# One causal-attention-and-experts kernel: scores by pairs of heads, transfers over two queues, later inverse deviations, fillers laid anew

## The reference, cut to what matters

```
x = x + skip(row_lstm(x))            # gated recurrence over the 16 rows, 48 features
t = tokens(x)                        # 16 images x 256 tokens x 96 channels
q, k, v = heads(ln(t) @ Wq, Wk, Wv)  # 6 heads of 16
s = (q . k) * 96**-0.5, causal       # 256 x 256 per image and head
t = t + (softmax(s) @ v) @ Wp + bp
g = softmax(ln(t) @ gate_w + gate_b), the best 2 of 4 kept and rescaled
t = t + sum_e g_e * (gelu(ln(t) @ w1_e + b1_e) @ w2_e + b2_e)    # 4 experts, hidden 384
```

## Time and profile before

| | us |
|---|---|
| median of 3 runs | 429.06 |
| lowest, highest | 427.37, 430.52 |
| profiled execution, its own time | 431.65 |
| its span, first to last instruction | 429.7 |
| mean granted TensorE clock | 0.987 |
| TensorE / weight loads busy | 404.0 / 332.1 |
| ScalarE / VectorE / GpSimd busy | 267.1 / 248.3 / 147.6 |

### The profile page before, as it was taken

How to read it: one execution, slowest core, us unless ns; L and a number is a source line. 1 busy time by engine, 2 the same in 40 slices (tenths; PEclk the granted TensorE clock), 3 DMA queues, 4 the chain that set the end, 5 groups by cost and what they waited for, 6 DMA issues and landing times.

```text
span 429.7 us, 10320 instructions
## 1 busy us (share of the span) xinstructions
PE 404.0 (94%) x3024; PEld 332.1 (77%) x3024; DVE 248.3 (58%) x867; ACT 267.1 (62%) x766; POOL 147.6 (34%) x314
## 2 busy tenths in 40 slices
PE   7999998887999899989998999899989998999996
PEld 4988984555588788868886888789777887787786
DVE  1576774475328753866386548645864585367425
ACT  3566652465486658665865686567747764877380
POOL 6000002366305631563155315532642254236200
PEclk9899999998899999999999999999999999999999
DMA  7700000310111012101200220021002100210000
GB/s 177 177 0 0 0 2 19 83 29 2 43 36 36 2 46 53 30 0 50 55 23 0 54 55 21 0 61 49 18 0 64 46 0 8 76 27 3 7 13 20
DMA packets 16472, 14.87 MB, mean 35 GB/s; under 512 B 7586, under 2 KB 13588, under 8 KB 16452
## 3 DMA queue, kind: packets, MB, share of 16 engines
q1 hardware_dynamic: 14644, 13.74, 12.4%
q10 hardware_dynamic: 1616, 0.74, 0.7%
q0 software_dynamic: 192, 0.15, 0.2%
HBM read 3.80 MB, written 1.57 MB: 12 GB/s over the span
## 4 chain that ended last, share of the span: by engine, by line
PE 72%; DVE 9%; issue 7%; POOL 6%; ACT 3%; DMA 1%; ACTq 1%; SPq 1%; POOLq 0%; DVEq 0%
PE F L1126 14%; PE T L1084 6%; PE A L1105 5%; PE F L1142 5%; PE F L1146 4%; PE F L1143 4%; PE F L957 3%; POOL p_sb L453 3%; PE S L1068 3%; PE S L1070 2%; ACT p_sb L598 2%; PE F L967 2%; DVE xh L770 2%; PE F L968 2%; PE S L1073 2%
## 5 line engine op out<-in xcount | busy, mean ns | idle before, releaser
L453 POOL TENSOR_SCALAR p_sb<-p_sb,rden 128x128 f32<-128x128 f32 (+1 forms) x192 | 79.5, 429 | 115.3 <-DVE rden L798 113.1
L1126 PE MATMUL F<-w_sb,hid 128*128 128x96 f32 x768 | 98.8, 272 | 0.0
L1126 PEld LDWEIGHTS F<-w_sb,hid 128*128 128x128 f32 x768 | 96.1, 192 | 0.0
L598 ACT ACTIVATE p_sb<-S,nmax 128x128 f32<-128x128 f32 (+1 forms) x192 | 78.9, 424 | 11.4 <-DVE nmax L792 11.4
L792 DVE TENSOR_REDUCE nmax<-S 128x2 f32<-128x512 f32 (+1 forms) x80 | 50.6, 632 | 51.5 <-PE S L1073 51.2
L1084 PE MATMUL T<-id_sb,p_sb 128*128 128x128 f32 x288 | 48.1, 286 | 12.3 <-POOL p_sb L453 10.4
L502 ACT COPY pt_sb<-T 128x512 f32<-128x512 f32 (+1 forms) x48 | 26.5, 551 | 44.6 <-PE T L1084 44.6
L644 ACT ACTIVATE hid<-F,b_sb 128x512 f32<-128x512 f32 x72 | 49.4, 689 | 7.0 <-PE F L1146 6.3
L1084 PEld LDWEIGHTS T<-id_sb,p_sb 128*128 128x128 f32 x288 | 31.5, 144 | 21.9 <-POOL p_sb L453 17.7
L598 ACT ACTIVATION_READ_ACCUMULATOR p_sb<-S,nmax 128x1 f32 x192 | 39.7, 207 | 0.0
L1068 PE MATMUL S<-k_bd,q_st 96*128 96x384 f32 (+2 forms) x96 | 38.1, 404 | 1.5 <-ACT p_sb L598 1.1
(11 more groups left out here) (151 smaller groups left out, 789.3 us busy)
## 6 DMA issues: line engine op xcount, KB each, us to landing
k_bd<-k_cur SPq DMA_DIRECT2D x93, 32.0 KB, 2.0
q_st<-q_cur SPq DMA_DIRECT2D x28, 96.0 KB, 2.3
k_bd<-k_cur SPq DMA_DIRECT2D x93, 16.0 KB, 1.8
t_st<-t_cm SPq DMA_DIRECT2D x7, 192.0 KB, 2.5
out_y<-y_sb SPq DMA_DIRECT2D x7, 192.0 KB, 1.9
x_pad<-in_x SPq DMA_DIRECT2D x2, 612.0 KB, 7.4
w_sb<-in_w SPq DMA_DIRECT2D x1, 576.0 KB
hid<-in_w SPq DMA_DIRECT2D x1, 576.0 KB, 6.8
```

The lines of the kernel that those rows point to most:

```text
L453: last = nc.gpsimd.tensor_scalar(p, p, rden[:, u % 3, i:i + 1], 1.0, ALU.mult, ALU.mult)
L598: last = nc.scalar.activation(p_sb[:, u % 3, i * nk:(i + 1) * nk], S[u % 2][:, i * nk:(i + 1) * nk], ACT.Exp, bias=nmax[:, u % 3, i:i + 1] ...
L1126: last = mm(dst[:, e * C:(e + 1) * C], hid[:, c, s * TT:(s + 1) * TT], w2_sb[:, c], start=False, stop=(c == NCH - 1), skip_group_check=True)
```

## The change

- A stationary set of queries now holds a pair of heads: 32 rows of high parts, 32 of low parts, 32 of high parts again (`PAIRS`, `PR`). The keys hold the high parts twice and the low parts once beside them, so all three terms come out of one product over 96 rows. A unit of two heads (256 keys) takes one product of 512 columns; a unit of three heads (128 keys) takes two, of 256 and 128 columns.
- `load_queries` takes a pair and issues two transfers for its high parts or one for its low parts; `load_keys` takes three heads and issues 6 for high or 3 for low parts, each over both images.
- In the steady state SP issues 9 transfers of queries and 6 of low keys, GpSimd the 12 of high keys, between its last `rstd2` and `keep_t1`. For block 0, ACT issues 9, SP 9 and GpSimd 9.
- `rstd2` moves from j = TILE_END+1 to the smaller of TILE_END+2 and 9, `normalize2` from TILE_END+2 to TILE_END+3, and that of the third tile behind the loop.
- FILL goes from 16, 3, 3, 2, 3, 3, 2, 1, 1, 2 to 12, 4, 3, 3, 3, 3, 3, 2, 1, 2; the sum stays 36.

```diff
--- before.py
+++ after.py
@@ -33,6 +33,7 @@
 HALF = B // 2
 HC = HALF * W
 HEADS, HS = 6, 16
+PAIRS, PR = HEADS // 2, 2 * HS
 VW = 32
 VB = 3 * VW + HS
 TT = 128
@@ -52,7 +53,7 @@
 NU = len(UNITS)
 TILE_END = [1 + max(u for u, (a, t, _) in enumerate(UNITS) if 2 * a + t == s) for s in range(SPB)]
 
-FILL = [16, 3, 3, 2, 3, 3, 2, 1, 1, 2]
+FILL = [12, 4, 3, 3, 3, 3, 3, 2, 1, 2]
 TAIL = SPB * NCH - sum(FILL)
 TAIL_EARLY = min(TAIL, 9)
 PT_ON_ACT = (1, 2, 4, 6, 8, 9)
@@ -136,10 +137,11 @@
         x1lo = sb("x1lo", [C, BT], F32R)
         x1f = sb("x1f", [C, BT])
         q_cur = sb("q_cur", [C, 2, BT], F32R)
-        q_st = sb("q_st", [C, 2, BT], F32R)
+
+        q_st = sb("q_st", [C, PAIRS, BT], F32R)
         k_cur = sb("k_cur", [C, 2, BT], F32R)
 
-        k_bd = sb("k_bd", [C, 2, 2, 2, 3, 2 * TT], F32R)
+        k_bd = sb("k_bd", [C, 2, PAIRS, 2, 2 * TT], F32R)
         v_cur = sb("v_cur", [128, SPB, 2, VB])
         nmax = sb("nmax", [128, 3, HG[0]])
         den = sb("den", [128, 3, HG[0]])
@@ -256,9 +258,12 @@
         t_staged = sem("t_staged")
         q_in = [sem("q_in0"), sem("q_in1")]
         q_in_first = [sem("q_in_first0"), sem("q_in_first1")]
-        kbd_in = [[sem(f"kbd_in{a}{g}") for g in range(2)] for a in range(2)]
+
+        khi_in = [sem("khi_in0"), sem("khi_in1")]
+        klo_in = [sem("klo_in0"), sem("klo_in1")]
+        k_first_sp = [sem("k_first_sp0"), sem("k_first_sp1")]
+        k_first_pool = [sem("k_first_pool0"), sem("k_first_pool1")]
         y_out = sem("y_out")
-        kbd_in_first = sem("kbd_in_first")
         idle_set = sem("idle_set")
         zeroed = sem("zeroed")
         w_dve = sem("w_dve")
@@ -274,8 +279,8 @@
 
             return x_pad[:, bass.ds(r0 * (B * PADW), B * PADW)].rearrange("p (b w) -> p b w", w=PADW)
 
-        KBD = 6 * 16
-        TRI = 3 * HS
+        Q_IN = (2 * 3 * 16, 3 * 16)
+        K_HI, K_LO = 6 * 16, 3 * 16
 
         def out_parts(slot):
 
@@ -313,42 +318,32 @@
         def queries_taken(eng, n, g):
 
             if isinstance(n, int) and n == 0:
-                eng.wait_ge(q_in_first[g], 32)
+                eng.wait_ge(q_in_first[g], Q_IN[g])
             else:
-                eng.wait_ge(q_in[g], 32 * n)
-
-        def keys_taken(eng, n, a, g):
-
-            if (a, g) != (0, 1):
-                eng.wait_ge(kbd_in[a][g], KBD * (n + 1))
-            elif isinstance(n, int) and n == 0:
-                eng.wait_ge(kbd_in_first, KBD)
+                eng.wait_ge(q_in[g], Q_IN[g] * n)
+
+        def keys_taken(eng, n, g):
+            if isinstance(n, int) and n == 0:
+                eng.wait_ge(k_first_sp[g], (K_HI, K_LO)[g])
+                eng.wait_ge(k_first_pool[g], (K_LO, K_HI)[g])
             else:
-                eng.wait_ge(kbd_in[a][g], KBD * n)
-
-        def load_queries(eng, g, taken, parts=(0, 1)):
-
-            for part in parts:
-                eng.dma_start(as_f32(q_st[part * TRI:(part + 1) * TRI, g, :]),
-                              as_f32(q_cur[g * TRI:(g + 1) * TRI, part, :])).then_inc(taken[g], 16)
-
-
-        def load_keys(eng, a, g, n=None):
-
-            taken = kbd_in_first if n is not None and (a, g) == (0, 1) else kbd_in[a][g]
-            cols = slice(a * 2 * TT, (a + 1) * 2 * TT)
-            if n is not None:
-                wait_alone(eng, khi_done, n + 1)
-            for below in ((True, False) if n is not None else (False, True)):
-                if n is not None and not below:
-                    wait_alone(eng, klo_done, n + 1)
-                for i in range(3):
-                    rows_h = slice((3 * g + i) * HS, (3 * g + i + 1) * HS)
-                    if below:
-                        dst, src = k_bd[TRI + i * HS:TRI + (i + 1) * HS, a, 0, g, i, :], k_cur[rows_h, 0, cols]
-                    else:
-                        dst, src = k_bd[i * HS:(i + 1) * HS, a, :, g, i, :], k_cur[rows_h, :, cols]
-                    eng.dma_start(as_f32(dst), as_f32(src)).then_inc(taken, 16)
+                eng.wait_ge(khi_in[g], K_HI * n)
+                eng.wait_ge(klo_in[g], K_LO * n)
+
+        def load_queries(eng, p, taken, low):
+
+            for row in ((PR,) if low else (0, 2 * PR)):
+                eng.dma_start(as_f32(q_st[row:row + PR, p, :]), as_f32(q_cur[p * PR:(p + 1) * PR, int(low), :])
+                              ).then_inc(taken[p // 2], 16)
+
+        def load_keys(eng, g, taken, low):
+
+            for h in range(3 * g, 3 * g + 3):
+                for row in ((2 * PR,) if low else (0, PR)):
+                    row += h % 2 * HS
+                    eng.dma_start(as_f32(k_bd[row:row + HS, :, h // 2, h % 2, :]),
+                                  as_f32(k_cur[h * HS:(h + 1) * HS, int(low), :].rearrange("p (a k) -> p a k", a=2))
+                                  ).then_inc(taken[g], 16)
 
 
         @block.sync
@@ -379,19 +374,23 @@
 
             def body(n, first=False, store=True, more=True):
                 if first:
-                    load_keys(sp, 0, 0, n)
+                    wait_alone(sp, khi_done, 1)
+                    load_keys(sp, 0, k_first_sp, False)
+                    wait_alone(sp, klo_done, 1)
+                    load_keys(sp, 1, k_first_sp, True)
                 else:
                     wait_alone(sp, scores_ready, NU * n)
+                    wait_alone(sp, qhi_done, n + 1)
+                    for p in range(PAIRS):
+                        load_queries(sp, p, q_in, False)
                     wait_alone(sp, qlo_done, n + 1)
-                    load_queries(sp, 0, q_in)
-                    load_queries(sp, 1, q_in)
+                    for p in range(PAIRS):
+                        load_queries(sp, p, q_in, True)
                     wait_alone(sp, klo_done, n + 1)
-                    load_keys(sp, 0, 0)
-                    load_keys(sp, 0, 1)
+                    for g in range(2):
+                        load_keys(sp, g, klo_in, True)
                 if store:
                     store_y(n - 2)
-                load_keys(sp, 1, 0)
-                load_keys(sp, 1, 1)
                 if more:
                     wait_alone(sp, tt_ready, n + 2)
                     stage(n + 2)
@@ -473,9 +472,15 @@
                     if j == EARLY_T0 + 1 and not last:
                         rstd1(n + 1)
                     for s in range(SPB - 1):
-                        if j == TILE_END[s] + 1:
+
+                        if j == min(TILE_END[s] + 2, NU - 1):
                             rstd2(n, s)
                 rstd2(n, SPB - 1)
+                if not last:
+                    wait_alone(pool, scores_ready, NU * n + NU)
+                    wait_alone(pool, khi_done, n + 2)
+                    for g in range(2):
+                        load_keys(nc.gpsimd, g, khi_in, False)
                 keep_t1(n, first)
                 if not last:
                     residual(n + 1)
@@ -484,7 +489,9 @@
             pool.wait_ge(w_in, 16 * N_WIN)
             rstd1(0)
             x1_whole(0)
-            load_keys(nc.gpsimd, 0, 1, 0)
+            wait_alone(pool, klo_done, 1)
+            load_keys(nc.gpsimd, 0, k_first_pool, True)
+            load_keys(nc.gpsimd, 1, k_first_pool, False)
             residual(0)
             body(0, first=True)
             with pool.Fori(1, NBLK - 1) as n:
@@ -628,9 +635,8 @@
                 heads_out(n, SPB - 1, first)
                 if not last:
 
-                    for a in range(2):
-                        for g in range(2):
-                            keys_taken(act, n, a, g)
+                    for g in range(2):
+                        keys_taken(act, n, g)
                     for g in range(2):
                         queries_taken(act, n, g)
                     take_q(n + 1)
@@ -649,11 +655,13 @@
             take_k(0)
             take_q(0)
             act.wait_ge(qhi_done, 1)
-            for g in range(2):
-                load_queries(act, g, q_in_first, parts=(0,))
+            for p in range(2):
+                load_queries(act, p, q_in_first, False)
             act.wait_ge(qlo_done, 1)
-            for g in range(2):
-                load_queries(act, g, q_in_first, parts=(1,))
+            for p in range(2):
+                load_queries(act, p, q_in_first, True)
+            load_queries(act, 2, q_in_first, False)
+            load_queries(act, 2, q_in_first, True)
             nc.scalar.copy(b2t[:], b2_sb[:]).then_inc(w_act, 1)
             act.wait_ge(w1_in, 16)
             nc.scalar.copy(w1hi[:], w1raw).then_inc(w_act, 1)
@@ -899,8 +907,9 @@
                     for s in range(SPB - 1):
                         if j == TILE_END[s] + 1:
                             attn_residual(n, s, first)
-                        if j == TILE_END[s] + 2:
+                        if j == TILE_END[s] + 3:
                             normalize2(n, s)
+                normalize2(n, SPB - 2)
                 if not first:
                     for s in range(sum(FILL[:-1]) // NCH, sum(FILL) // NCH):
```

(15 more changed lines are left out.)

## The result

The changed kernel takes **439.8 us** (median of 4 runs, 435.55 to 443.7) beside 428.24 for the kernel before, measured along with it (4 runs, 427.37 to 430.52). The ratio is **1.018 [1.0129, 1.0231]**: slower, by 1.3 to 2.3%. It leaves out two of the four runs (442.25 and 443.7), in which TensorE's clock was granted at 0.969 and 0.965 in the mean; the others had 0.988 (435.55, the profiled one) and 0.984 (437.35).

The account below looks back on a forecast made before the run. The prediction took a chain through all engines, with VectorE's order deciding, as the bound. On the profiled 431.65, +3.5 (seven blocks), -0.7 (block 0) and +3.5 (start) gave 438.0; the same +6.3 on the median 429.06 gave 435.4 us, range 420 to 440.

Parts of the forecast that it names:

- Products removed: Score products on TensorE: fewer of them save 1.9 us a block, 15 us in eight, if nothing else binds.
- T(8): TensorE's probability transposes of unit 8, middle block: start at 315.6, as before (315.54), after GpSimd's scaling ends at 315.5.
- recip(7): VectorE's step before GpSimd's scaling of unit 7: at 312.8, 0.6 us later, since combine(1) and normalize2(0) move ahead of it.
- T(0) to T(5): TensorE's probability transposes of units 0 to 5, middle block: 0.70 us earlier at first, 0.5 next, last at 309.0 against 309.96.
- T(9): TensorE's probability transposes of unit 9, middle block: 317.6 against 316.96, 0.6 us later, as rstd2(1) stands between two scalings.
- The period: Length of a middle block, 41.7 us before: +0.5 us, bounds -0.3 and +0.8; +3.5 over seven blocks.
- The start: ACT's first query transfers before b2t: five more at 0.7 us each delay the first exponentials, +3.5 us (+2.9 to +5).
- Block 0: First block's loop, without fillers or combine: earlier scalings and fewer score products give -0.7 us, bounds 0 and 1.9 saved.
- Transfers later: Later blocks' key and query transfers on GpSimd and SP: cost nothing, hidden before project_v with 3 us to spare.
- Rival 4: TensorE's clock also falls in the longer start: some 7 us at the lower level cost about 3, 438.5 us; chance 0.08.
- Rivals 1 and 2: First: TensorE bounds, all 1.9 comes through, 418.7 us, chance 0.12. Second: part comes through, 425.6 us, chance 0.22.
- rival 3: Nothing moves in the loops and the longer issue is partly covered: 429 to 432 us; chance 0.16.

Follow-up runs that it names:

- e3: Changed kernel with the fillers, rstd2 and normalize2 as before the change, so only the head pairs and two queues stay: 427.27 us, ratio 0.9989.
- e11: Kernel before the change, with only the second tile's rstd2 moved behind the scaling of unit 9 and its normalize2 to j=9: 425.01 us, ratio 0.9914.
- e8: e3 with the second tile's rstd2 moved behind the scaling of unit 9 and its normalize2 to j=9: 423.58 us, ratio 0.989.
- e5: Changed kernel with combine(1) alone moved back to j=4 in VectorE's order: 429.14 us, ratio 0.9992.
- e6: Kernel before the change with combine(1) alone moved from j=4 to j=5: 443.5 us, ratio 1.034.
- e1: Changed kernel with the old FILL, all else as changed: 428.65 us, ratio 1.0007.
- e2: Changed kernel with rstd2 and normalize2 at their old places, the new FILL kept: 441.48 us, ratio 1.0286.
- e7: Changed kernel with idle products in TensorE's waits before T(7), T(8) and T(9) of the blocks after the first: 437.93 us, ratio 1.0226.
- e10: Changed kernel with each later block's 12 high-key transfers put back on SP instead of GpSimd: 501.93 us, a single run.
- e4: Changed kernel with ACT's copies b2t and w1hi put ahead of its last five query transfers: 437.4 us, ratio 1.0251.
- e9: e8 with the first query transfers shared, ACT issuing 4 and SP 5, and 40 idle products instead of 32: 422.95 us, ratio 0.986.
- e12: e9 with more idle products before block 0 and in every step of its loop: 420.2 us, ratio 0.9802.

## Why the prediction was right, and where not

It said slower, 435.4 us, by VectorE's order. The mechanism is shown; several sizes were off, and they partly cancelled. That the total fits so well is luck in part, as the entry on the sum says.

- **Products removed.** 1.9 us a block by rows; 0.73 came through with all else as before (e3: 41.67 to 40.94), 0.66 beside the better place of the deviation (e11 to e8: 41.21 to 40.55). The rest is waiting, as T(8)'s 1.17 us in e3. The forecast had a lead that ends at recip(7), and no product saving beyond: right for the changed kernel.
- **T(0) to T(5).** Forecast 297.74, 299.5, 309.0; came 297.74, 299.55, 309.34. This is the step that failed in size: "309.96 - 0.98 = 309.0". The lead was 0.62. At T(4) it was 0.44 and not 0.5, and of the two savings between T(4) and T(5) the 0.23 of the scores came, but not the "wait of about 0.25 before the channel transposes": they follow T(4) by 0.78 us, where they followed it by 0.73. TensorE before, and after:

```profile
306.31 0.61 PE L1084 MATMUL T<-id_sb,p_sb 128*128 128x128 f32 x4
307.04 0.65 PE L1034 MATMUL M<-id_sb,xh 128*96 128x128 f32 x4
```

```profile
308.04 0.66 PE L1090 MATMUL T<-id_sb,p_sb 128*128 128x128 f32 x4 [0.16 <-POOL p_sb L452]
308.82 0.68 PE L1043 MATMUL M<-id_sb,xh 128*96 128x128 f32 x4
```

  The 0.34 that is missing runs through all that follows.
- **recip(7).** Forecast 312.8, came 313.11; it follows T(5) by 3.77 as forecast (3.76). e5 and e6 show that combine(1) in that place is the cause: 1.3 us a block in either direction, as it was costed (1.26).
- **T(8).** Forecast 315.6, came 315.95. recip(8) was at 314.53 instead of 314.3, scale(8) ended at 315.79, and behind it TensorE still waited 0.16 us, by the row for VectorE's copy of T(7), which had come late with recip(7). I had followed scale(8) alone.
- **T(9).** Forecast 317.6, came 317.89, the same 0.3 later. What rstd2(1) between the scalings costs depends on what it is held against: 0.24 a block, with normalize2(0)'s move in it, against its old place in front of both (e1 against e3, after against e2), where it made T(8) late instead, and 0.63, with that move too, against a place behind both (e1 against e8). Neither reaches its 0.98.
- **The period.** Forecast +0.5, within -0.3 and +0.8; came +0.77 (41.67 to 42.44). By the runs: pairs -0.73, deviations +0.24, place of combine(1) +1.32, the rest of the fillers' places -0.06.
- **The start.** +3.5 forecast, +2.5 came. In this profile the five added transfers cost 0.49 each (6.48 - 4.01 over 5), below the lower end of 0.59 that I had taken from SP. It is the lowest of eight: with the same nine issues the profiles of e1, e2, e3, e5, e7, e8 and e10 show 6.75 to 7.29 us, and first exponentials 12.1 to 12.6 us after the keys' low part, so the forecast of 0.7 each was nearer than this one execution tells. How much the chain over b2t leads the queries behind it (e4) is 0.6 us by this profile and up to 1.4 by the others.
- **Block 0.** -0.7 forecast, with 0 and -1.9 as bounds; -2.1 came, which is outside them. Part of it is the clock: from the first exponentials on, after has 3.4 us at the lower level in this block and before 6.8. e6 tells how much: its block 0 has the code of before and, like after, 3.4 us at the lower level, and it took 40.10 us. Beside after's 39.15 that is -0.95, near the forecast; the rest, 1.2 us, goes with the longer fall in before.
- **Transfers later.** Free, as forecast: 0.51 us an issue, 2.6 us to spare (3 forecast). But "cost nothing" was said of SP's issue time too, on the ground that it is covered. e10 shows that this cover is the second queue's doing. The Trainium skill ("DMA: Bandwidth & Descriptors", Rules for kernel authors) says that spreading over queues saves only issue time; e10 agrees, and here issue time decides: with all 27 on one queue the run took 501.93 us instead of 439.8, the falls of the clock that came with it included.
- **The sum.** Profiled execution against profiled execution it is +3.9 (435.55 against 431.65), where +6.3 was forecast: in spans the loops with the last block cost 5.6 instead of 3.5, start and block 0 together 0.4 instead of 2.8, and 1.9 went off in the recurrence, where only before's clock fell, which no term of the sum knew of. The ratio's +1.8% is +7.7, and the median 439.8 is +11.6, just inside the stated 420 to 440. That 435.4 lies so near the profiled 435.55 is luck. The profiled run is at the low end: three more of the changed kernel had 437.35 to 443.7 at clocks of 0.984 to 0.965.
- **The clock.** Rival 4 had the clock as a mishap of block 0, and a fall in the longer start is in the profile as it said (clock 0.78 in 80 to 84 us). The runs show the clock as a cost of the loop too: after's fall at 232 to 236 us made its period 43.13 instead of 42.44, and in e2 and e6, falls in four and five of six periods cost 1.2 to 1.3 us each. The changed kernel, e2, e4 and e6, the kernels at full pace with such falls, all have combine(1) at j=5, a wait of about 1.2 us before T(7) and another of 0.7 to 1.2 before T(8). In the twelve periods of these four with a fall, it begins 23.1 to 24.6 us after v, behind the wait before T(7) (T(7) stands at 21.6 to 22.3) and within 0.8 us of T(8). e1, e3, e5, e8, e9, e11, e12 and before, without the 1.2 us before T(7), show no fall in their loops, though before and e3 wait 1.1 to 1.2 us ahead of T(8); neither does e7, which fills the wait. This is one profile of each kernel, and the clocks of e7's other runs (0.979 to 0.992) don't tell where they fell, so the link is well supported but not proved. I had priced the late T(7) as time alone; by these profiles it costs clock too. The Trainium skill ("TensorE: Matmul & The Clock Gate", Why this matters for your kernels) has pauses between bursts bring the lower clock. It means longer pauses than the waits of 0.7 to 1.2 us in these loops, so the trace agrees only in kind; e12, with products in the pauses of block 0, at clock 1.0, agrees from the other side.

Rivals 1 and 2 fell: no kernel with combine(1) at j=5 came under 41.67 a period. With the fillers as they were, rival 3 (429 to 432) would have been about right (e1, 428.65).

## What to carry to other kernels

When work is moved on a busy engine (filler parts), look at what in-order code on **other** engines hangs on it: here 1.3 us of VectorE's work changed its place by one step, and that ate all that fewer products gave. An operation whose result is wanted late goes behind the last of a row of urgent ones, not between two of them. A wait on TensorE is to be priced twice, as time and as clock, and idle products in the waits, above all in the first block, are cheap where the engine is idle anyway (e7: 42.40 against 42.44 a period).

## What was not expected of the hardware

- TensorE's granted clock falls in stretches where the profile shows it busy for most of the time: 3.46 of 4.00 us at a clock of 0.57 (after, 232 to 236 us). The busy figure is itself made at the slower rate, so it isn't the share before the fall; what is shown is only that such blocks hold a wait of 1.2 us before T(7), and that the fall comes behind it. One fall cost 0.7 to 1.3 us in the loop.
- How much of a run is at the lower level changes from run to run of the same code, 435.55 to 443.7 us at mean clocks of 0.988 to 0.965. With idle products in every step of block 0 (e12) six runs agreed within 0.7 us.
- An engine's issue of a small transfer took 0.51 us on GpSimd (6.11 / 12), 0.49 to 0.7 at the margin on ACT, by the profile, and 0.64 on SP (11.47 / 18); 27 on one queue set the time of the whole kernel (e10).
- One score product of 512 columns in the place of four (0.56 us) or two saved less than half of its rows' time on the clock, since the transposes behind it wait for GpSimd and VectorE: of 1.9 us a block, 0.7.
